# Splitting the transposed probabilities before, instead of after, the maximum of the newest scores

## What is computed

```
x = x + 0.5 * ffn(layernorm(x))
x = x + attention(layernorm(x))
x = x + 0.5 * ffn(layernorm(x))

attention(x):                      # 16 heads of 128
  q, k, v = x @ wq, x @ wk, x @ wv
  q, k = rope(q) / sqrt(128), rope(k)
  logits = q @ k.T, masked causally
  probs = softmax(logits)
  return (probs @ v) @ wo
```

## Time and profile before

| | |
|---|---|
| median of three executions | 1540.08 us |
| the profiled execution | 1538.69 us, of which the span of the trace is 1536.9 us |
| granted TensorE clock, mean | 0.99 of full speed |
| PE busy | 1443.2 us (94%) |
| DVE busy | 1148.8 us (75%) |
| ACT busy | 946.2 us (62%) |
| POOL busy | 808.4 us (53%) |
| PE's share of the chain that ended last | 78%; DVE 12% |
| one unit of the attention | some 29.8 us |

### The profile page before, as it was taken

How to read it: one execution, slowest core, us unless ns; L and a number is a source line. 1 busy time by engine, 2 the same in 40 slices (tenths; PEclk the granted TensorE clock), 3 DMA queues, 4 the chain that set the end, 5 groups by cost and what they waited for, 6 DMA issues and landing times.

```text
span 1536.9 us, 25917 instructions
## 1 busy us (share of the span) xinstructions
PE 1443.2 (94%) x8992; PEld 1273.1 (83%) x8992; DVE 1148.8 (75%) x2536; ACT 946.2 (62%) x1951; POOL 808.4 (53%) x731
## 2 busy tenths in 40 slices
PE   5799999789999999999999999999999987999998
PEld 4678778679899899989989998998999875878776
DVE  7778878877776777777777767777767777787786
ACT  4444544577776777677677667767777644444443
POOL 4636346355556555555555555555555533633644
PEclk9999999999999999999999999999999998999999
DMA  4000000200000000000000000000000020000000
GB/s 165 1 0 1 0 1 1 69 8 8 15 8 9 14 8 8 15 1 14 16 1 9 22 1 8 22 2 8 8 1 1 4 108 1 1 14 1 14 14 14
DMA packets 10832, 23.67 MB, mean 15 GB/s; under 512 B 849, under 2 KB 4945, under 8 KB 10577
## 3 DMA queue, kind: packets, MB, share of 16 engines
q1 hardware_dynamic: 10704, 22.04, 4.4%
HBM read 19.94 MB, written 2.10 MB: 14 GB/s over the span
## 4 chain that ended last, share of the span: by engine, by line
PE 78%; DVE 12%; issue 5%; POOL 2%; ACT 2%; DMA 0%; DVEq 0%; POOLq 0%; ACTq 0%
PE ps L1179 23%; PE ps L1181 22%; PE ps L1180 22%; PE ps L1469 9%; DVE ps L1109 2%; DVE up_act L966 2%; DVE pT_l L309 1%; DVE hid L981 1%; POOL w_l L309 1%; DVE hid L976 1%; ACT up_act L656 1%; DVE x_sb L910 1%; DVE base_gate L951 1%; DVE stats L812 0%; PE ps L1280 0%
## 5 line engine op out<-in xcount | busy, mean ns | idle before, releaser
L581 POOL TENSOR_SCALAR probs<-probs,inv_sum 128x128 f32<-128x128 f32 (+7 forms) x256 | 212.3, 829 | 385.6 <-DVE inv_sum L1065 385.5
L1109 DVE CUSTOM_DVE_ANT_0 ps<-ps,causal 128x128 f32<-128x128 f32 (+7 forms) x256 | 194.9, 761 | 212.4 <-PE ps L1181 210.7
L759 ACT ACTIVATE probs<-ps,neg_max 128x128 f32<-128x128 f32 (+7 forms) x256 | 189.1, 739 | 74.6 <-DVE neg_max L1109 74.5
L309 DVE TENSOR_TENSOR pT_l<-ps,pT_h 128x512 fp32r<-128x512 f32 (+3 forms) x384 | 200.6, 549 | 3.4 <-ACT pT_h L738 3.2
L738 ACT ACTIVATE pT_h<-ps 128x512 fp32r<-128x512 f32 (+3 forms) x384 | 174.2, 490 | 39.0 <-PE ps L1469 36.5
L570 POOL TENSOR_TENSOR rot_sin<-swapped,rope 128x512 f32<-128x512 f32 x128 | 165.2, 1290 | 55.7 <-ACT swapped L715 52.8
L1469 PE MATMUL ps<-ident,probs 128*128 128x128 f32 x1152 | 171.1, 276 | 23.4 <-DVE pT_l L309 19.2
L1180 PE MATMUL ps<-pT_l,v_h 128*128 128x256 f32 (+1 forms) x640 | 180.1, 281 | 0.0
L1181 PE MATMUL ps<-pT_h,v_l 128*128 128x256 f32 (+1 forms) x640 | 180.0, 281 | 0.0
L1179 PE MATMUL ps<-pT_h,v_h 128*128 128x256 f32 (+1 forms) x640 | 178.7, 279 | 1.2 <-DVE oA_l L309 1.2
L309 POOL TENSOR_TENSOR hid_l<-hid,hid_h 128x512 fp32r<-128x512 f32 (+1 forms) x88 | 114.2, 1297 | 99.3 <-ACT hid_h L658 99.3
(11 more groups left out here) (183 smaller groups left out, 4328.5 us busy)
## 6 DMA issues: line engine op xcount, KB each, us to landing
w_raw<-attn_w SPq DMA_DIRECT2D x32, 256.0 KB, 2.6
w_in<-ffn_w SPq DMA_DIRECT2D x10, 744.0 KB, 9.1
x_sb<-x_in SPq DMA_DIRECT2D x4, 512.0 KB, 5.5
out<-x_sb SPq DMA_DIRECT2D x4, 512.0 KB, 2.9
rope<-rope_w SPq DMA_DIRECT2D x1, 1024.0 KB, 7.2
expand_raw<-expand_w SPq DMA_DIRECT2D x2, 384.0 KB, 12.3
```

The lines of the kernel that those rows point to most:

```text
L309: return eng.tensor_tensor(dst, src, high.bitcast(F32), ALU.subtract)
L581: pool.tensor_scalar(probs[s % 4][:, 0:n], probs[s % 4][:, 0:n], inv_sum[:, s % 4:s % 4 + 1], 1.0, ALU.mult, ALU.mult).then_inc(probs_read ...
L759: act.activation(probs[t % 4][:, 0:a * n].rearrange("p (a n) -> p a n", a=a), view, ACT.Exp, bias=neg_max[:, t % 4:t % 4 + 1], scale=-1.0, ...
L1109: dve.tensor_tensor_reduce(out=view, in0=view, in1=causal[:, SEQ - a * n:].rearrange("p (a n) -> p a n", a=a), scale=-SCALE, scalar=HUGE, ...
```

## The change

In each step of the attention the block that makes the low halves of tile t - 3 is moved on DVE ahead of the maximum of t. Each instruction, its operands and its waits stay the same. The orders of PE, ACT, POOL and SP are unchanged.

```diff
                     if t % 2 == 1:
                         invert_sum(p, t, first)
-                    if t < STEPS:
-
-                        view, a, n = score_view(t % 2, t % SEQ_TILES)
-                        dve.wait_ge(scores_done, STEPS * p + t + 1)
-                        dve.nop(nofuse=True)
-                        dve.tensor_tensor_reduce(out=view, in0=view,
-                                                 in1=causal[:, SEQ - a * n:].rearrange("p (a n) -> p a n", a=a),
-                                                 scale=-SCALE, scalar=HUGE, op0=ALU.add, op1=ALU.min,
-                                                 accum_out=neg_max[:, t % 4:t % 4 + 1]).then_inc(max_done, 1)
-                    if first and t < 2:
-
-                        rope_sum(2 + t, 2 + t)
-                        rope_low_part(dve, 2 + t, 0, 2 + t)
-                    if first and t == 0:
-                        layer_norm_low(2 * CHUNKS - 1, CHUNKS - 1)
                     tile = tile_of_step(p, t, T_LAG + 1, first)
                     if tile:
                         q, s = tile
...
                             low(dve, pT_l[i // 2 % 2][:, slot:slot + count, half:half + P],
                                 ps[:, bank, 0:P * count].rearrange("p (a b) -> p a b", a=count),
                                 pT_h[i // 2 % 2][:, slot:slot + count, half:half + P]).then_inc(pT_ready, 1)
+                    if t < STEPS:
+
+                        view, a, n = score_view(t % 2, t % SEQ_TILES)
+                        dve.wait_ge(scores_done, STEPS * p + t + 1)
+                        dve.nop(nofuse=True)
+                        dve.tensor_tensor_reduce(out=view, in0=view,
+                                                 in1=causal[:, SEQ - a * n:].rearrange("p (a n) -> p a n", a=a),
+                                                 scale=-SCALE, scalar=HUGE, op0=ALU.add, op1=ALU.min,
+                                                 accum_out=neg_max[:, t % 4:t % 4 + 1]).then_inc(max_done, 1)
+                    if first and t < 2:
+
+                        rope_sum(2 + t, 2 + t)
+                        rope_low_part(dve, 2 + t, 0, 2 + t)
+                    if first and t == 0:
+                        layer_norm_low(2 * CHUNKS - 1, CHUNKS - 1)
                     side = side_work(p, t, first, last)
```

More of the change, by code:

```diff
@@ L1103, in attention @@
                         invert_sum(p, t, first)
+                    tile = tile_of_step(p, t, T_LAG + 1, first)
+                    if tile:
+                        q, s = tile
+                        i = s % SEQ_TILES
+                        half = P * (i % 2)
+                        for n, (slot, count) in enumerate(tile_groups(i)):
+                            dve.wait_ge(pT_high, groups_before(q, s) + n + 1)
+                            bank = T_BANK + (GROUPS_AT[i] + n) % 2
+                            low(dve, pT_l[i // 2 % 2][:, slot:slot + count, half:half + P],
+                                ps[:, bank, 0:P * count].rearrange("p (a b) -> p a b", a=count),
+                                pT_h[i // 2 % 2][:, slot:slot + count, half:half + P]).then_inc(pT_ready, 1)
                     if t < STEPS:
@@ L1118, in attention @@
                         layer_norm_low(2 * CHUNKS - 1, CHUNKS - 1)
[L1119 to L1129, removed]
                     side = side_work(p, t, first, last)
```

## The result

The changed kernel takes 1570.32 us (median of four executions, 1569.23 to 1575.31), the kernel before beside it 1540.06 us. The ratio is 1.0204, with a 95% interval from 1.0181 to 1.0226: slower by 30.3 us. I had forecast 1574 us, slower by 34. The granted TensorE clock is 1.00 of full speed over the middle stretch, 400 to 1200 us, in both kernels, so it has no part in the loss there.

What follows compares the result with a forecast made beforehand. The prediction took PE to bound the attention; 15 crossings at 1.04 us and 15 at 1.2 give 33.6 us, ends 0, so 1538.69 becomes 1572.3, plus 1.4 for the median: 1574 us, range 1558 to 1584.

Steps and rivals of the forecast that it cites:

- The bound: In the attention's middle, PE is all but full, with one small hole per unit, 12.8 us in all.
- The chain: ACT and DVE run alternately, each waiting for the other; transposes of step 1 come 1.04 us later per unit.
- The old hole: PE's 0.49 us hole before step 7's transposes closes but is spent again at the bank just before: net +0.11 us.
- two bounds: PE's price per crossing into the next unit lies between a gain of 0.79 us and a loss of 1.96 us.
- Odd units: Units without weight split in or about step 7: transposes of step 1 1.04 us late; 15 crossings, 15.6 us.
- Unit 2: Even unit with a weight split in step 5: transposes of step 1 worked out as 1.30 us late.
- Unit 0: Even unit without a weight split in step 5: loss taken as 1.2 us, as for all 15 even units (18.0 us).
- The ends: First and last unit and the drain behind it: taken at 0 within 2 us.
- The signs: In the changed profile, PE's holes before step 7's transposes vanish; waits of about 1 us appear in step 1, some 30 us.
- In phase again at step 5: By step 5 PE, ACT and DVE are in phase again, 1.04 us late; DVE had idled 3.50 us there.
- The gain: Rival, chance 0.08: step 7's hole closes and ACT and DVE keep up; 19 us faster, 1521 us.

Runs made afterwards that it cites:

- The last kernel: Against the kernel before: low halves ahead in steps 1 to 5 and 7, later swap of step 0, ACT's weight splits behind the high halves; 1514.51 us, ratio 0.9840.

## Why the prediction was right

**The bound.** PE bound the attention before, with one small hole per unit: right. The last kernel shows its size: with the hole and the chain's other waits removed, a unit takes 28.92 to 29.06 us.

**The chain.** The prediction's central step, that ACT and DVE become one closed chain which ends at the transposes of step 1, is right in each of its events to 0.03 us (table above, odd unit). The run with steps 6 and 7 and that with only step 7 met the numbers which the same chain gives for them. Cutting the swap out of it gave the odd units back all but 0.03 us of their loss, or all but 0.15 against the control.

**The old hole.** Closed in step 7 and paid again at the bank just before, net +0.11: measured +0.08.

The prediction had also called its 1.04 to 1.2 us "near the middle" of its two bounds, a gain of 0.79 and a loss of 1.96. The middle is a loss of 0.59, so the bounds gave no support to the number; the chain did.

**Odd units**, 1.04 us each: measured 30.85 - 29.82 = 1.03. **Unit 2**, worked out at 1.30: measured 1.29.

**Unit 0.** Here is the term that was mis-sized. I took 1.2 us for all 15 even units, on the ground that in half of them the low halves start "a bit ahead of the scores". Unit 0 lost 0.77. The step that I missed is in step 5: the moved low halves leave 0.31 us less between the maximum of step 5 and the low halves of step 6. In the odd units that is swallowed by the wait for the values' high half, in unit 2 by the weight split on ACT. Only in unit 0 does it go on. The run with step 5 left alone shows it: there unit 0 loses 1.06, so step 5 is 0.29 of the 0.43 by which 1.2 was too much. The other 0.14 is there because 1.2 stood for the mean of both even units. Seven such units at 0.43 less are 3.0 us; the seven units 2, at 1.29 instead of the 1.2 taken, give 0.6 back.

**The ends.** I took them at 0 within 2 us. In the profiled executions the span grew by 32.1 us. 15 odd units of 1.03, seven units 2 of 1.29 and seven units 0 of 0.77 are 29.9 us. The very first unit, for which I had counted a loss as well, is 0.4 us shorter, the last crossing 0.65 shorter; 0.95 us more lie before the first unit's step 5, and 1.9 behind that of the last. Together +1.8. The remaining 0.4 is one odd unit that took 31.20 us. Why the first unit gained was not tried. So part of the nearness of the forecast is luck: the units were counted some 4 us too dear, and the ends, with the one odd unit, gave 2.6 us back that were in no term.

**The signs.** The holes before the transposes of step 7 are gone in odd and even units, and the one in step 1 is about 1 us. The prediction did not have the waits of 0.28 us in step 0 of the even units; over the whole span PE's wait for low halves is 37.8 us (before 19.2), where "some 30" was said for the attention. They add nothing to the loss, since the start in step 1 does not depend on PE.

**In phase again at step 5.** Right for the changed kernel. It is a narrow thing, though: with the swap of step 0 moved by one step it failed, and cost units 0 and 2 some 0.4 and 0.7 us.

**What the chain did not tell.** In the prediction the exponential of step 7 is late by the maximum. With only step 6 moved, the same delay takes another way, through PE's values and DVE's wait for them. In the full change that way is shorter than the one through the maximum and does not show. A replay of a chain is only good for the order that it was made for; for the next order each engine's row has to be gone through again.

**The rivals.** The gain needed the high halves early in DVE's idle time; in step 7 DVE now idles 1.68 us for them, so they were not. The rule of the Trainium skill (Perfetto Trace Analysis, Optimization Strategies) which spoke for a gain named the right wait, but the run with only step 7 moved, which serves exactly this wait, is 0.7% slower. The move of step 7 was part of a gain only beside the later swap and splits.

## What to carry to other kernels

When one engine idles before an instruction, ask whether what is moved into that idle time waits for an engine that itself waits for that instruction. If so, two engines that ran side by side become one chain, and all that both do adds up. This costs nothing where the bound engine's next demand has room, as in steps 1 to 5 here, and is paid for where it has none. Before moving, follow the chain through one full period with spacings from the trace, engine by engine, until each engine is back in phase; the loss may show several steps behind the place that was changed. If it is a loss, look at what stands on the chain without need (here a swap and two weight splits) and move that first: then a part of the same edit, six of the eight steps here, can pay.

## What the runs showed of the hardware

A rotation sum of DVE, both of whose inputs lie in SBUF, takes 0.68 us in most places, but in the run with only step 6 moved one took 1.39, in unit 2. DVE's row, and POOL's beside it:

```profile
753.86 1.39 DVE L1052 TENSOR_TENSOR rot<-rot,rot_sin 128x512 f32<-128x512 f32 x1
```

```profile
753.68 1.02 POOL L581 TENSOR_SCALAR probs<-probs,inv_sum 128x896 f32<-128x896 f32 x1
```

POOL ends at 754.70, DVE 0.55 us later, at 755.25. The same sum in the kernel before took 0.90 us:

```profile
747.18 0.90 DVE L1052 TENSOR_TENSOR rot<-rot,rot_sin 128x512 f32<-128x512 f32 x1
```

```profile
746.53 1.02 POOL L581 TENSOR_SCALAR probs<-probs,inv_sum 128x896 f32<-128x896 f32 x1
```

It ends 0.53 us after POOL's end at 747.55. It is no chance of two rows: of 126 such sums in the kernel before 39 took 0.75 us or more, and each of these began while a POOL instruction ran and ended 0.53 to 0.55 us after it. The reverse shows too: 18 sums that are listed 0.03 to 0.06 us behind the start of a POOL instruction took their 0.68 or 0.69 us, and POOL's scaling took some 0.88 us instead of 0.37 for 128 columns and 1.10 instead of 0.58 for 384. So of two such instructions one seems to wait until the other is through. The Trainium skill, SBUF — State Buffer, section SBUF: two separate sides, names such a lock between a DVE instruction with two SBUF inputs and a GpSimd one that reads SBUF; these rows agree with it.

It makes the time of an instruction depend on what another order puts beside it, and I have not followed it in the prediction. In the run with only step 6 moved it accounts for what the even units lost. Measured from the maximum of step 5, the rotation sum of step 0 in unit 2 starts as before (9.96 against 9.95 us). But POOL's scaling beside it starts 0.48 later, since POOL's work before it waited for the late swap of step 6. The sum takes 0.49 longer, the cosine product and the high halves of step 1 come 0.50 and 0.49 later, and the transposes of step 1 0.32 later: this is the 0.33 us of unit 2. In unit 0 the sum takes 1.16 instead of 0.81 us and the transposes come 0.09 later, of the 0.10 lost. This is read from the traces; no run took it apart.
